# Moving the early routing of twelve tiles one to two chunks forward in the last sequence of a macaron block (FFN, recurrent attention, FFN) on one core

## The reference, cut to what matters

```
x = x + 0.5 * ffn(layernorm(x))       # top-1 mixture of 8 experts, 128 -> 512 -> 128
x = x + attn(layernorm(x))            # 4 sequences of 512 tokens, 8 heads of 64, gated recurrence
x = x + 0.5 * ffn(layernorm(x))       # the same mixture again

def ffn(x):                           # per token
    logits = x @ w_router             # 8 logits
    sel = argmax(softmax(logits)); wgt = softmax(logits)[sel]
    return wgt * (relu(x @ w1[sel] + b1[sel]) @ w2[sel] + b2[sel])
```

## Time and profile before

| | us |
|---|---|
| median of 3 runs | 426.08 (424.91 to 426.52) |
| the profiled execution, its time | 429.1 |
| the profiled execution, its span | 427.3 |
| PE busy in the span | 375.8 |
| DVE busy | 316.3 |
| ACT busy | 236.5 |
| POOL busy | 122.1 |

### The profile page before, as it was taken

The page is one execution under the profiler, slowest core; times in us unless marked ns, Lnnn a source line. Parts: engine busy times, 40 slices in busy tenths (PEclk is TensorE's granted clock), DMA queues, the critical chain, the costliest instruction groups (busy, mean ns, idle before and its releaser), DMA issues.

```text
span 427.3 us, 11335 instructions
## 1 busy us (share of the span) xinstructions
PE 375.8 (88%) x3628; PEld 301.4 (71%) x3629; DVE 316.3 (74%) x1007; ACT 236.5 (55%) x634; POOL 122.1 (29%) x123
## 2 busy tenths in 40 slices
PE   8147999977999999999999999999989866879991
PEld 5117999723687787887878878778768733679990
DVE  7833777653658898878989788988789994658780
ACT  3734656611546767467684567655556912646550
POOL 2333543077001111103110120111031168334552
PEclk9566999996999999999999999999999989889997
DMA  7996223111799997876730000000002612323320
GB/s 171 392 316 237 68 71 59 38 43 44 151 179 188 187 176 184 180 181 153 185 92 0 0 0 0 0 0 0 2 2 60 228 62 83 117 69 90 98 67 1
DMA packets 57089, 44.57 MB, mean 104 GB/s; under 512 B 4063, under 2 KB 53857, under 8 KB 56673
## 3 DMA queue, kind: packets, MB, share of 16 engines
q1 hardware_dynamic: 54018, 38.14, 37.5%
q0 software_dynamic: 2752, 5.73, 4.8%
q10 hardware_dynamic: 288, 0.31, 0.4%
HBM read 17.98 MB, written 25.73 MB: 102 GB/s over the span
## 4 chain that ended last, share of the span: by engine, by line
PE 68%; ACT 9%; DVE 7%; issue 6%; DMA 4%; POOL 2%; another core or an unknown queue 1%; POOLq 0%; ACTq 0%; SPq 0%; DVEq 0%
PE bank L960 64%; ACT WVT L837 3%; DMA xn_rows<-XN 2%; POOL slots L531 2%; DMA XB<-xn_rows,IDX 1%; DVE ST L1508 1%; ACT XN L659 1%; PE bank L1086 1%; PE bank L1343 1%; ACT E L846 1%; ACT W1R L857 1%; DVE QS L2111 1%; PE bank L1244 1%; DMA XN<-slots 1%
## 5 line engine op out<-in xcount | busy, mean ns | idle before, releaser
L599 POOL TENSOR_TENSOR HS<-HS,MHALF 128x8 f32<-128x8 f32 x16 | 26.4, 1647 | 130.6 <-DVE HS L2161 130.6
L737 ACT ACTIVATE HT<-bank,W1R 128x128 f32<-128x128 f32 x138 | 40.6, 365 | 21.3 <-issue 11.0
L960 PE MATMUL bank<-XBT,W1R 128*128 128x128 f32 x368 | 51.9, 286 | 0.1
L960 PE MATMUL bank<-W,HT 128*128 x368 | 50.1, 280 | 0.5 <-issue 0.5
L960 PEld LDWEIGHTS bank<-XBT,W1R 128*128 128x128 f32 x368 | 47.2, 201 | 0.8 <-issue 0.4
L960 PEld LDWEIGHTS bank<-W,HT 128*128 128x128 f32 x368 | 46.1, 197 | 1.0 <-issue 0.7
L837 ACT ACTIVATE WVT<-bank,AC 128x128 f32<-128x128 f32 x128 | 36.5, 375 | 11.7 <-PE bank L960 11.3
L960 PE MATMUL bank<-MASKB,IDB 128*128 128x512 bf16 x111 | 35.7, 424 | 7.9 <-DVE CREDIT L1960 5.2
L801 ACT ACTIVATE QKT<-bank,COLS 128x512 f32<-128x512 f32 x32 | 22.0, 687 | 28.9 <-PE bank L960 28.9
L545 POOL DMA_INDIRECT XB<-xn_rows,IDX x23 | 22.6, 984 | 32.9 <-PE bank L1086 19.9
L584 POOL DMA_INDIRECT out<-YB,IDX x23 | 22.6, 983 | 25.8 <-DVE YB L1794 17.4
(11 more groups left out here) (377 smaller groups left out, 989.0 us busy)
## 6 DMA issues: line engine op xcount, KB each, us to landing
slots<-FILL SPq DMA_DIRECT2D x74, 258.0 KB
W<-w SPq DMA_DIRECT2D x2, 2048.0 KB, 12.3
XN<-slots SPq DMA_DIRECT2D x23, 129.0 KB
W<-w SPq DMA_DIRECT2D x1, 2064.0 KB, 7.9
y_rows<-YB SPq DMA_DIRECT2D x23, 64.0 KB
X<-x SPq DMA_DIRECT2D x4, 256.0 KB, 5.3
xn_rows<-XN SPq DMA_DIRECT2D x2, 512.0 KB, 8.8
XN<-X SPq DMA_DIRECT2D x1, 768.0 KB, 5.1
```

The lines of the kernel that those rows point to most:

```text
L599: g.tensor_tensor(HS[:, 3, :], HS[:, 2, :], MHALF[:, 0:H], ALU.pow).then_inc(roots_ready, 1)
L737: ins = a.activation(HT[:, j % 2, c, :], bank[2 + j % 2][:, c * P:(c + 1) * P], ACT.Relu, bias=W1R[:, j % 2, F + c:F + c + 1])
L960: return t_.matmul(o, l, r, start=start, stop=stop, skip_group_check=True)
```

## The change

In the last sequence only:

- PE: the transposes for q = 0 and 1 go from the end of chunk 2 to the end of chunk 0; those for q = 2, and the logits for q = 0 and 1, from chunk 3 to the end of chunk 1; the logits for q = 2 from chunk 3 to chunk 2, behind its scores; the ranks from chunk 3 to the end of chunk 2.
- ACT: the copies follow the transposes (end of chunk 0, end of chunk 1). Seven of the twelve normalisations and the exponentials go to the end of chunk 2; five stay at the end of chunk 3.
- DVE: `shift(1, 0)` goes from chunk 2 to chunk 1, and `early_choice()` from chunk 3 to chunk 2, behind `variance(b, 1)`.
- The order of bank uses and one wait follow.

No instruction is added or taken away.

```diff
-        LAST_USES = [*PJ_USES, "xt0", "xt1", "xt2", "lg", "rk"]
+        LAST_USES = [*PJ_USES[0:20], "xt0", "xt1", *PJ_USES[20:24], "xt2", "lg", *PJ_USES[24:28], "rk"]
...
 # ACT
-            def layer_norm(f, group):
+            def layer_norm(f, group, lo=None, hi=None):
                 act.wait_ge(shift_ready[f], group + 1)
-                for t in range(*GROUPS[f][group]):
+                first, end = GROUPS[f][group]
+                for t in range(lo or first, hi or end):
...
-                if last and c == 3:
-                    xn_channels(1, 2)
...
                 elif last:
-                    layer_norm(1, 0)
+                    layer_norm(1, 0, UNDER_XN1)
...
-                if last and c == 2:
+                if last and c == 0:
                     xn_channels(1, 0)
                     xn_channels(1, 1)
+                if last and c == 1:
+                    xn_channels(1, 2)
+                if last and c == 2:
+                    layer_norm(1, 0, 0, UNDER_XN1)
+                    exponentials(1, 0, EARLY)
...
 # PE
-                if last and c == 3:
-                    xn_channels(1, 2)
+                if last and c == 2:
+                    early_logits(2)
...
                 if last and c == 3:
-                    early_logits(0)
-                    early_logits(1)
                     state_decays(b, c)
...
-                if last and c == 3:
-                    early_ranks()
                 values(b, c)
-                if last and c == 2:
+                if last and c == 0:
                     xn_channels(1, 0)
                     xn_channels(1, 1)
+                if last and c == 1:
+                    xn_channels(1, 2)
+                    early_logits(0)
+                    early_logits(1)
+                if last and c == 2:
+                    early_ranks()
...
 # DVE
                     scale_q(b, 3)
-                    early_choice()
...
+                if last and c == 2:
+                    early_choice()
...
-                if last and c == 2:
+                if last and c == 1:
                     shift(1, 0)
```

More of the change, by code:

```diff
@@ L49 @@
 AMID = 6
+UNDER_XN1 = 7
 REGION = NT
@@ L650, in xn_channels @@
                 a.activation(XNT[:, q, :], bank[q % 2][:, :], ACT.Copy).then_inc(done, 1)
-            def layer_norm(f, group):
+            def layer_norm(f, group, lo=None, hi=None):
                 act.wait_ge(shift_ready[f], group + 1)
-                for t in range(*GROUPS[f][group]):
+                first, end = GROUPS[f][group]
+                for t in range(lo or first, hi or end):
                     if f == 1 and t == NT - 2:
                         exponentials(1, EARLY, NT)
-                    if f == 1 and t == 8:
-                        exponentials(1, 0, EARLY)
                     a.activation(XN[f][:, t, 0:D], x_at(f, t), ACT.Identity, scale=LNA[:, 5, t:t + 1],
@@ L974, in xn_channels @@
                 if f == 1 and q == 3:
-                    pe.wait_ge(*pj_read_at(NB - 1, "lg"))
+                    pe.wait_ge(*pj_read_at(NB - 1, "s3"))
                 elif f == 1:
@@ L1384, in chunk @@
                     head_gates(b + 1)
-                if last and c == 3:
-                    early_logits(2)
-                elif more:
+                if more:
                     state_decays(b, c)
```

## The result

The changed kernel took 431.93 us in the median of 4 runs (430.53 to 435.07), the kernel before beside it 425.63 us; the ratio is 1.0146, 95% interval [1.0100, 1.0192]. A second comparison later gave 1.0158 [1.0100, 1.0215]. That is some 6.3 us slower, where 2.0 us and a range up to 430.3 us were forecast.

What follows compares the result with a forecast made beforehand. PE was taken to bound chunk 2 and DVE chunk 3, making kernel time POS plus a constant. POS + 2.13 + 1.80 - 1.80 - 0.13 = + 2.0 us took 426.08 to 428.1 us, range 425.2 to 430.3.

Steps and rivals of the forecast that it cites:

- What bounds, and that nothing behind POS gives time back: Last sequence: PE sets the pace in chunk 2, DVE in chunk 3; kernel time is POS plus a constant.
- The sign set for the whole tail: From POS to the end: 83.7 us of the span, to stay the same to half a us.
- First pair of transposes: nothing.: Transposes q = 0 and 1 at the end of chunk 0: hidden in waits of chunk 1, 0.1 us at most.
- PE's insert ahead of v3: Chunk 2: transposes q = 2 and all logits make ACT's squares 2.1 to 2.2 us late; 2.13 in the sum.
- The choice, ahead of QS: DVE, chunk 2: adds 1.80 us; QS ends at 331.2 instead of 327.27, PE waits 1.7 us at `from_state`.
- the sum: POS: + 2.13 (squares late) + 1.80 (choice in) - 1.80 (choice out) - 0.13 = + 2.0 us.
- The clock: PE in chunk 3: new waits of 1.5 to 1.9 us; granted clock kept at 1.00, POS at + 2.0.
- the rival: Clock falls in chunk 3: POS 1.3 to 1.7 us later still, + 2.0 + 1.5, 429.6 us; chance 0.14.
- the faster one: Chunk 2: DVE's idle 1.1 us is filled if ACT's squares start before 325.6; 425.0 us, chance 0.11.
- the one of a tail that does not hang on POS: Behind POS: up to 2.0 us hidden in something that does not move; no change, 426.1 us, chance 0.13.
- more handovers than I counted: Four rearranged engines: waits for copies, choice, bank and ranks together add + 1.2; 429.3 us, chance 0.12.

Runs made afterwards that it cites:

- e4_first_pair: Kernel before, with only the transposes q = 0 and 1 and their copies moved to the end of chunk 0; ratio 0.9987.
- e5_logits_only: Changed kernel, ACT copying the logits out of bank 1, with choice, ranks, normalisations and exponentials back in chunk 3; ratio 1.0054 to the kernel before.
- e1_copy_out: Changed kernel, but ACT copies the logits out of bank 1 and DVE chooses from the copy; ratio 1.0065 to the kernel before.
- e6_spin: Changed kernel, with 17 dummy matmuls in PE's wait ahead of o3; ratio 1.0094 to the kernel before.
- e3_copy_out_choice_first: Changed kernel, with logits copied out of bank 1 by ACT and DVE's choice ahead of the variance of chunk 1; ratio 1.0002 to the kernel before.

## Why the prediction was wrong

The measured 431.93 us lie outside the range. Its steps, one by one:

- *What bounds, and that nothing behind POS gives time back:* right as far as the times tell. Every shift of POS in the table lies inside the interval of the measured ratio, and from POS to the first block read the length is the same (20.76 us against 20.74). The sign set for the whole tail, half a us, was too fine: 81.9 us against 83.7.
- *First pair of transposes: nothing.* Right: POS - 0.10 us in e4_first_pair.
- *PE's insert ahead of v3, 2.13 us:* right in size. DVE waited 2.62 us for the squares, and e5_logits_only puts its effect on POS at 2.03 us.
- *The choice, ahead of QS:* **this is the step that failed.** It said "PE comes to `from_state` at 327.42 + 2.15 = 329.6, and stands there until about 331.3: a new wait of 1.7 us". That takes PE as running freely from v3 to `from_state`. Between the two stands o3, in the bank that the logits now hold. The runs showed PE idle for 4.27 us there. That puts QS 2.6 us later than the sum had it, and the halved clock behind the wait another 1.5 us. The front of this document says that `pj_wait` makes PE wait for the reader of the use two places before, and the diff moves "lg" to the place two before "o3"; the sum did not follow the new list through to the uses behind it. The sum priced what the moved instructions wait for, and not whom the unmoved ones now wait for.
- *The clock:* the rival took it for chunk 3, at 1.5 us. The clock did fall to 0.50 in chunk 3, in e1_copy_out too, where `from_state` at 340.05 took 1.55 us against 0.95; there it cost POS nothing, for POS is + 1.92, below the sum's + 2.0. What cost 1.5 us was the clock in chunk 2, behind the wait that I had missed. There the slow products stood on the path. That the rival named the same 1.5 us is chance, for its place and its reason were others. By the Trainium skill ("TensorE: Matmul & The Clock Gate", section "What's actually happening") activity lifts the slow default; with dummy matmuls in the wait the traces agree, 1.05 us against 1.91 for the same product.

How the 6.02 us add up. From the mark, QS of chunk 2 came at 28.04 us against 20.02 before, + 8.02. PE reached o3 2.2 us late (the insert), started it another 4.5 us late (the wait), and took 3.15 us instead of 1.67 up to the state decays (the clock, 1.5): 8.2, of which ACT and DVE took up 0.1 to 0.2. From QS to POS it then took 14.98 us instead of 16.98, since the choice (1.80) and the shift are not there any more and DVE waits nowhere: 8.02 - 2.00 = 6.02. My sum had 3.93 for QS, and e1_copy_out measured that. The clock adds 1.5 (e6_spin), and the 2.6 that are left are the bank's turn.

| kernel | mark | POS | POS from the mark, against before | ratio measured |
|---|---|---|---|---|
| before | 306.56 | 343.56 | | |
| after | 303.76 | 346.78 | + 6.02 | 1.0146 |
| after, once more | 304.27 | 347.38 | + 6.11 | 1.0158 |
| after, choice one operation later | 305.01 | 348.81 | + 6.80 | 1.0138 |
| after, dummy matmuls in the wait | 305.27 | 346.78 | + 4.51 | 1.0094 |
| logits copied out | 305.12 | 344.04 | + 1.92 | 1.0065 |
| only transposes and logits forward, copied out | 304.29 | 343.32 | + 2.03 | 1.0054 |
| after, choice first | 304.46 | 342.44 | + 0.98 | 1.0017 |
| copied out, choice first | 304.59 | 341.83 | + 0.24 | 1.0002 |
| only the first pair | 304.27 | 341.17 | - 0.10 | 0.9987 |

The numbers on POS are from one trace each. Taken as a share of 426 us it lies inside the interval of the measured ratio in every row (+ 6.80 is 1.60%, + 1.92 is 0.45%, - 0.10 is - 0.02%). The rivals of the prediction: the faster one fell (its condition, squares not late, did not hold), the one of a tail that does not hang on POS fell (the kernels whose POS is later are slower by as much, within the intervals), and the one of "more handovers than I counted" had the right sign and none of the size, because it was not a mechanism but a remainder. It should have been one: a shared bank's turn.

## What to carry to other kernels

When a step that uses a shared buffer in turn moves forward, the uses behind it in that buffer are the ones to look at: each now waits for the moved step's reader, although neither it nor its line in the diff has changed. Follow that reader back through its own engine's order; if it stands behind something that needs the waiting engine, the wait holds all the work of that loop. Here two cures worked without undoing the move: to let the reader go first in its own queue (two groups of instructions changed places, worth some 5 us), and to let an idle engine empty the buffer at once (0.25 us of ACT). Neither made the change a gain: the best of these, with both, has a ratio of 1.0002.

## What the runs showed that I had not expected

Two executions of one length can hide a difference. The profiled spans differ by 1.4 us where the medians differ by 6.3, because the profiled execution of the kernel before reached the mark 2.8 us later, and from the first block read to the end took 427.3 - 364.30 = 63.0 us against 428.7 - 367.54 = 61.2, both in work that the change does not touch. The executions of the kernel after also differ among themselves, from 430.53 to 435.07 us, and the profiled one is the fastest of them. A mark inside the changed stretch brought the traces and the times together.

The granted clock fell in chunk 3 of e1_copy_out after two short waits, of 1.29 us and, at the row of 340.05 shown above, of 1.85 us, where in the kernel before waits of 0.33 and 1.22 us left it at 1.00. The first of the two in its PE timeline:

```profile
336.86 0.40 PE L967 MATMUL bank<-M,SELQ 128*128 128x128 bf16 x4 [1.29 <-ACT WVT L838]
```

and its busy time in the half us in which the second wait began, and in half a us behind it:

```profile
338.00:338.50 0.50, 0.20 (x2) 0.01 (x1) 0.50 (x2) 0.50 (x4) 0.00 (x0) 1.00 0.05 16
...
340.00:340.50 0.50, 0.45 (x4) 0.48 (x4) 0.50 (x2) 0.50 (x2) 0.00 (x0) 0.50 0.00 0
```

The clock was at 1.00 when the second wait began and at 0.50 behind it. The length of the waits alone does not decide when it falls. e3_copy_out_choice_first has the same two waits, 1.29 us and 1.85, and there the same product still took the 0.95 us that it takes at a granted clock of 1.00 (PE's timeline):

```profile
334.64 0.40 PE L967 MATMUL bank<-M,SELQ 128*128 128x128 bf16 x4 [1.29 <-ACT WVT L838]
...
337.84 0.95 PE L967 MATMUL bank<-CS,QS 64*128 64x65 f32 x28 [1.85 <-DVE QS L2117]
```

In that trace the clock fell only behind this product: the granted clock is still 1.00 from 338.50 to 339.00 and is 0.50 from 340.00. So two equal waits halved the clock at different moments, and no run here shows what decided it.
